# Step products of a prologue in four column groups, and the prologue's order

## The chip, the cores and the metric

The kernel runs on one core of one Trainium2 chip. The metric is the device time of one execution in microseconds (us); less is better. Times of before and after are medians of several runs; the profile is of one more execution.

## What is computed

Sixteen sequences of 512 tokens with 128 features pass through one layer: a state-space mixer, a residual with a layer norm, a mixture of eight experts of which each token takes two, a residual and a layer norm. What matters here is the head of the mixer:

```python
zxbcdt = x @ Win.T
z = zxbcdt[..., :D_INNER]                        # 256 columns
xBC = zxbcdt[..., D_INNER:D_INNER + CONV_DIM]    # 512 columns
dt = zxbcdt[..., D_INNER + CONV_DIM:]            # 4 columns, the steps
xBC = silu(conv(xBC) + conv_b)                   # 4 taps along the tokens
dtp = softplus(dt + dt_bias)
dA = exp(dtp * -exp(A_log))
# then a scan over the tokens, norm, gate, Wout
```

The router's logits `u @ centroids.T` (8 columns) are taken partly from x as well: the kernel folds the part that comes straight from x into the same product, so that the step product of a sequence has 4 + 8 = 12 columns (`DT`).

## The kernel before, in words

Five queues are written out by hand (`block.tensor`, `scalar`, `vector`, `gpsimd`, `sync`), each in its own fixed order, tied by semaphores. Each engine works in program order; what its next instruction waits for holds up all behind it. The work goes in slots: slot -1 is the prologue, slots 0 to 15 each scan one sequence (four chunks of 128 tokens), project the next, and route the one before. Then come 135 expert tiles and the final norm.

The prologue (`enter_all` of TensorE and ScalarE, the first branch of `slot_dve`) has to do three things. It turns all sixteen x blocks: `enter_x(q)` is four transposes on TensorE (L546) into bank p5 or p7, which ScalarE copies to xT (L841). It makes the step products of all sixteen sequences: `enter_dt(q)` on TensorE (L560) has a chunk of xT as the standing operand and `w_dt`, padded from 12 to 96 columns (`PADN`), as the moving one, four chunks a sequence and two passes a chunk, so eight passes. Their results lie in banks p6 (sequences 0 and 1), pl[1] (2 to 9) and p4 (10 to 15), as `dt_place` says; VectorE adds the bias to the four step columns (L1147), and ScalarE copies the eight gate columns (L865, `keep_gates`). And it projects sequence 0: `project_block` (L511) for each of four blocks, ScalarE's first tap (L902, `tap0`), three more taps on VectorE (L1131), `activate` (L908), `skip_part` (L913), z blocks (L519), `gate_part` (L924), `inner_products` (L647), `keep_products` (L919).

The softplus of the steps is fourteen small VectorE instructions in a chain (`softplus_step`, L1161 to L1183), preceded by ScalarE's Abs and Exp (L847, L849). It is done in two groups: sequences 0 and 1 (`G0 = 2`) in the prologue, since the first scans need them, and 2 to 15 in slot 0, five steps after each of its first chunks. `sums` on TensorE (L597), `decay` on ScalarE (L857) and `split` on VectorE (L1196 to L1199) follow each group, then `turn_parts` (L524) and `exponents` (L532 to L537) make the mask exponents of a chunk. Slot 0's first mask is VectorE's L1207: it waits for the inner products' copy and for the exponents.

SyncE issues the x blocks in order (L407 to L415) and loads the expert weights after the second z block. GpSimd makes constants in the prologue.

Of the kernel before, what the change touches and what calls it, by code (L numbers as in the profile page):

```python
# [27 lines left out]
P = 128  # L28
SEQS, TOKS = 16, 512
NC = TOKS // P  # L30
H, HD = 4, 64
# [9 lines left out]
G1 = 10  # L41
# [14 lines left out]
SP_STEPS = 13  # L56
LN_STEPS = 2
GATE_STEPS = 6
G0 = 2
# [6 lines left out]
ON_POOL = 1  # L66
FIN = 4
# [23 lines left out]
def build(nc, t, out):  # L91
    ctx = ExitStack()
    with ctx:
# [17 lines left out]
        w_dt = sb("w_dt", [P, PADN])  # L111
# [167 lines left out]
        gates_in = sem("gates_in")  # L279
        fold_psum = sem("fold_psum")  # L280
# [72 lines left out]
        def dt_place(q):  # L353

            if q < G0:
                return p6, NC * DT * q
            if q < G1:
                return pl[1], NC * DT * (q - G0)
            return p4, P + NC * DT * (q - G1)

        def dt_block(lo, hi):

            o, at = dt_place(lo)
            return o[:, at:at + (hi - lo) * NC * DT].rearrange("p (c e) -> p c e", e=DT)
# [140 lines left out]
        def _(pe):  # L505
# [35 lines left out]
            def enter_x(q):  # L541

                pe.wait_ge(seq_in[q], 16)
                wait(pe, xT_ready, q - 1)
                for c in range(NC):
                    mm = pe.transpose((p5, p7)[q % 2][:, c * P:(c + 1) * P], land[q][:, c, :], ident[:, :])  # L546
                mm.then_inc(xT_psum, 1)

            def enter_dt(q):

                pe.wait_ge(xT_ready, q + 1)
                if q == 0:
                    pe.wait_ge(const_step, 3)
                if q == G1:
                    pe.wait_ge(decays_ready, 1)
                    pe.wait_ge(parts_ready, 1)
                o, first = dt_place(q)
# [43 lines left out]
            def enter_all():  # L601
# [6 lines left out]
                enter_dt(0)  # L608
                project_block(q, 0)
                enter_dt(1)  # L610
                project_block(q, 1)
                enter_x(2)
                for k in range(3, SEQS):
                    enter_x(k)
                    enter_dt(k - 1)
                    if k == 5:
                        pe.wait_ge(const_ready, CONSTS)
                        pe.wait_ge(a_ready, 1)
                        sums(0, G0, (upto, after, ones), 1)
                        project_block(q, 2)  # L620
                    elif k == 7:
                        pe.wait_ge(parts_ready, 1)
                        pe.wait_ge(v_ready, 1)
                        pe.wait_ge(gates_in, 1)
                        turn_parts(q, p6[0:KS, P:2 * P])
                        project_block(q, 3)
                    elif k == 9:
                        pe.wait_ge(picks_made, 1)
                        exponents(q, 0)
                    elif k == 11:  # L630
                        pe.wait_ge(w_in, 16 * W_LOADS)
                        z_block(q, 0)
                enter_dt(SEQS - 1)
                pe.wait_ge(S_ready, 1)
                z_block(q, 1)
                inner_products(q)
                pe.wait_ge(v_ready, 2)
                pe.wait_ge(gates_in, 3)
# [47 lines left out]
            def slot_pe(s, scan, project, route):  # L686
# [4 lines left out]
                for c in range(NC):  # L691
                    tok = slice(c * P, (c + 1) * P)
                    n = NC * s.n + c
                    if scan and c != 1 and (c + 1 < NC or project):
                        if not route and c == 0:
                            pe.wait_ge(v_ready, 2)
                            pe.wait_ge(gates_in, 2)
# [23 lines left out]
                    if project and c == 1:  # L721
                        if q.n == G0:
# [103 lines left out]
        def _(act):  # L826
# [16 lines left out]
            def enter_dt(g, lo, hi):  # L843

                w = (hi - lo) * NC * H
                act.wait_ge(v_ready, g + 1)
                act.activation(ev[:, 0:w], v[:, 0:w], ACT.Abs).then_inc(abs_done, 1)  # L847
# [980 lines left out]
```

## Time and profile before

| | us |
|---|---|
| median of 3 runs | 707.19 |
| the runs | 703.23, 707.2, 707.19 |
| the profiled execution | 704.99 |
| its span, from the first instruction to the last | 703.2 |
| TensorE busy | 638.3 (91%) |
| VectorE busy | 539.3 (77%) |
| ScalarE busy | 478.9 (68%) |
| GpSimd busy | 467.3 (66%) |

All times in rows are us from the span's start. A pass is one MATMUL of the profile; a matmul of 32-bit floats has two, a transpose has one. The engines are called PE (TensorE), ACT (ScalarE), DVE (VectorE), POOL (GpSimd) and SP (SyncE); PEld is the load of the standing operand. A matmul's end is modelled, so in a stream of passes the start-to-start distance is what each costs.

### The profile page before, as it was taken

What the parts mean: (1) busy time and instruction counts of PE and PEld (TensorE: products, weight loads), DVE (VectorE), ACT (ScalarE), POOL (GpSimd) and SP (SyncE); (2) the same over time, 40 slices, a digit from 0 to 9 for tenths busy, and PEclk for the clock granted to TensorE, in tenths of its full rate; (3) what the DMA queues carried; (4) which work ended last, traced back from release to release, by engine and by line L of the source; (5) the groups of instructions that cost most, each with busy time, mean ns of one, the idle gap of its engine ahead of it and who ended that gap; (6) DMA issues with size and microseconds to landing.
All of it is one profiled execution on the core that took longest, in us unless ns stands there. A gap on an engine that the chain in (4) does not pass through costs nothing.

```text
span 703.2 us, 19658 instructions
## 1 busy us (share of the span) xinstructions
PE 638.3 (91%) x4891; PEld 519.3 (74%) x4891; DVE 539.3 (77%) x1845; ACT 478.9 (68%) x1211; POOL 467.3 (66%) x696
## 2 busy tenths in 40 slices
PE   6978999999999999999998689999999999999900
PEld 5856666666666656666666489999999999999900
DVE  3468988889888998889889667776666666878744
ACT  3757778777878778777887367665566556677824
POOL 5012468787878878788777757777745545777754
PEclk9999999999999999999999999999999999999965
DMA  9280001101111011101110123323422223556253
GB/s 251 51 296 20 2 27 36 46 29 35 36 42 47 25 34 35 47 28 38 32 43 32 40 59 86 92 79 108 98 78 72 71 70 102 165 155 190 104 188 111
DMA packets 56668, 54.50 MB, mean 77 GB/s; under 512 B 9562, under 2 KB 45918, under 8 KB 56304
## 3 DMA queue, kind: packets, MB, share of 16 engines
q1 hardware_dynamic: 45840, 33.67, 17.4%
q0 software_dynamic: 8416, 16.93, 7.1%
q10 hardware_dynamic: 2304, 2.65, 1.1%
q8 instruction: 44, 0.72, 0.4%
q14 instruction: 64, 0.52, 0.3%
HBM read 31.05 MB, written 22.63 MB: 76 GB/s over the span
## 4 chain that ended last, share of the span: by engine, by line
PE 69%; issue 8%; POOL 6%; ACT 6%; DVE 5%; DMA 3%; SPq 1%; DVEq 0%; ACTq 0%; POOLq 0%
PE p L682 14%; PE pl L673 10%; PE pj L511 5%; PE p L673 5%; PE p L771 4%; PE p L746 3%; PE p L717 3%; PE p L792 3%; PE p L740 3%; PE p L757 3%; POOL moe_rows L1749 2%; PE pj L519 2%; PE pj L665 2%; PE p L647 2%; PE p L519 1%
## 5 line engine op out<-in xcount | busy, mean ns | idle before, releaser
L1749 POOL DMA_INDIRECT moe_rows<-xT x135 | 134.6, 997 | 79.6 <-DVE xT L1374 51.9
L1673 POOL DMA_INDIRECT sorted_rows<-pair,slot x128 | 128.8, 1007 | 30.6 <-issue 28.4
L1131 DVE SCALAR_TENSOR_TENSOR acc<-pj,conv_w_sb,acc 128x511 f32<-128x511 f32 (+2 forms) x192 | 141.2, 735 | 7.3 <-ACT acc L902 5.3
L682 PE MATMUL p<-w,xT 128*128 x1080 | 143.5, 276 | 3.2 <-ACT xT L1048 3.0
L1048 ACT ACTIVATE xT<-pl,b_sb 128x128 f32<-128x128 f32 x360 | 102.9, 369 | 48.0 <-PE pl L673 46.0
L682 PEld LDWEIGHTS p<-w,xT 128*128 128x128 f32 x1080 | 131.4, 192 | 4.3 <-issue 4.3
L673 PE MATMUL pl<-xT 128*128 128x128 f32 x720 | 95.1, 275 | 1.6 <-DVE xT L1362 1.6
L673 PEld LDWEIGHTS pl<-xT 128*128 128x128 f32 x720 | 87.5, 192 | 1.9 <-issue 1.9
L1370 DVE TENSOR_TENSOR xT<-p,b_sb 128x128 f32<-128x128 f32 x135 | 39.3, 291 | 64.5 <-PE p L682 60.4
L1048 ACT ACTIVATE xT<-p,b_sb 128x128 f32<-128x128 f32 x180 | 51.6, 371 | 23.8 <-PE p L673 23.6
L902 ACT ACTIVATE acc<-pj,conv_b_sb,conv_w_sb 128x512 f32<-128x512 f32 x64 | 49.7, 777 | 25.1 <-PE pj L511 24.2
L511 PE MATMUL pj<-xT,w_xbc 128*128 128x512 f32 x128 | 66.5, 601 | 0.0
L740 PEld LDWEIGHTS p<-M,Xdt 128*64 128x64 f32 x512 | 26.8, 136 | 47.1 <-issue 45.3
L1686 POOL TENSOR_TENSOR Xdd<-Xdt,cur 128x256 f32<-128x256 f32 x48 | 29.5, 615 | 48.0 <-DVE Xdt L1406 34.9
L1362 DVE COPY xT<-w 128x512 f32 x135 | 59.0, 437 | 0.1
L1636 POOL TENSOR_TENSOR gt<-yv,sz 128x256 f32<-128x256 f32 x64 | 47.1, 736 | 11.0 <-DVE yv L1426 10.3
L1207 DVE TENSOR_TENSOR M<-pl,Gm 128x512 f32<-128x512 f32 x64 | 43.9, 686 | 11.6 <-issue 10.1
L1374 DVE SCALAR_TENSOR_TENSOR xT<-xT 128x128 f32<-128x128 f32 x135 | 48.1, 356 | 4.7
L837 ACT ACTIVATE pl<-pl 128x512 f32<-128x512 f32 x64 | 37.2, 582 | 19.5 <-PE pl L537 19.3
L673 PE MATMUL p<-xT 128*128 128x128 f32 x360 | 47.6, 275 | 0.0
L740 PE MATMUL p<-M,Xdt 128*64 128x128 f32 x512 | 42.1, 285 | 5.8 <-issue 4.9
L673 PEld LDWEIGHTS p<-xT 128*128 128x128 f32 x360 | 43.7, 192 | 0.0
(235 smaller groups left out, 1360.6 us busy)
## 6 DMA issues: line engine op xcount, KB each, us to landing
xT<-sorted_rows SPq DMA_DIRECT2D x135, 65.0 KB, 1.9
xres<-in_x SPq DMA_DIRECT2D x16, 256.0 KB, 3.0
w<-in_w SPq DMA_DIRECT2D x2, 2048.0 KB, 10.1
acc<-moe_rows SPq DMA_DIRECT2D x12, 256.0 KB, 3.2
xT<-moe_rows SPq DMA_DIRECT2D x12, 256.0 KB, 5.5
out<-sz ACTq DMA_DIRECT2D x10, 256.0 KB, 2.1
moe_rows<-xT POOLq DMA_INDIRECT x135, 2.5
sorted_rows<-pair,slot POOLq DMA_INDIRECT x128, 2.4
```

Source lines behind the costliest of these rows:

```text
L511: pe.matmul(pj[k % 2][:, :], w_xbc[:, k * P:(k + 1) * P], xT[:, q.n, :], start=True, stop=True).then_inc(proj_psum, 1)
L673: mm = pe.matmul(h_bank[j % 3][:, f * P:(f + 1) * P], w1e[j % 4][:, f * P:(f + 1) * P], sT[j % 4], start=True, stop=True)
L682: mm = pe.matmul(y_bank(j)[:, 0:P], hT[j % 4][:, f, :], w2[:, bass.ds(e, 1), f, :].rearrange("p e d -> p (e d)"), start=(f == 0), stop=(f ...
L740: mm = pe.matmul(p7[half, (h // 2) * P:(h // 2 + 1) * P], Xdt[c % 2][:, h * HD:(h + 1) * HD], M[c % 2][:, h, :], start=(h < 2), stop=(c == ...
L902: act.activation(acc[:, c, :], pj[c % 2][:, :], ACT.Identity, bias=conv_b[:, c:c + 1], scale=conv_w[:, c, TAPS - 1:TAPS]).then_inc(tap0_do ...
L1048: act.activation(hT[j % 4][:, f, :], h_bank[j % 3][:, f * P:(f + 1) * P], ACT.Gelu, bias=b1[:, bass.ds(e * FB + f, 1)]).then_inc(hT_ready, 1)
L1131: ins = dve.scalar_tensor_tensor(out=acc[:, k, j:TOKS], in0=pj[k % 2][:, 0:TOKS - j], scalar=conv_w[:, k, TAPS - 1 - j:TAPS - j], in1=acc[ ...
L1362: dve.tensor_copy(w1e[j % 4], w1[:, bass.ds(expert[j], 1), :].rearrange("p e f -> p (e f)")).then_inc(w1e_ready, 1)
L1374: dve.scalar_tensor_tensor(out=ye[j % 8], in0=ye[j % 8], scalar=xs[k][:, P + 1:P + 2], in1=xs[k][:, 0:P], op0=ALU.mult, op1=ALU.add).then_ ...
L1636: pool.tensor_tensor(gt[:, :, c * P:(c + 1) * P], yv[c % 2][:, :, :], sz[s.par][:, :, c * P:(c + 1) * P], ALU.mult).then_inc(g_ready, 1)
L1673: pool.indirect_dma_start(out=sorted_rows[:, :], out_offset=bass.IndirectOffsetOnAxis(slot[q.par][:, c, k:k + 1], 0), in_=(rowA, rowB)[k][ ...
L1749: pool.indirect_dma_start(out=moe_rows[:, :], out_offset=bass.IndirectOffsetOnAxis(xs[k][:, P:P + 1].bitcast(I32), 0), in_=ye[j % 8], in_o ...
```

## The change

The step product is turned round: `w_dt`, now padded from 12 to 32 columns, stands, and the 512 tokens of a sequence move. Four sequences go into four groups of 32 columns of the array and so to four groups of 32 partitions of one bank, pl[1] (`steps_of`). ScalarE copies the bank to `turned` (`keep_steps`), TensorE turns it in four transposes into p6 (`turn_steps`), and VectorE takes both the steps with their bias and the gates from there. Softplus groups are now sequences 0 to 3 and 4 to 15. The three orders of the prologue are written anew; VectorE copies two of the turned x blocks (13 and 15) in ScalarE's place; nine of the second softplus's fourteen steps stand at the end of the prologue, the other five in slot 0 after chunk 0; Abs and Exp of the second group move from slot 0 to the prologue.

```diff
-G1 = 10
+GROUP = 4
+SP_AHEAD = 9
-G0 = 2
+G0 = GROUP
+X_MOVED = (13, 15)
-        w_dt = sb("w_dt", [P, PADN])
+        w_dt = sb("w_dt", [P, Q])
+        def by_seq(ap):
+            return ap.rearrange("p (c n e) -> p n c e", c=NC, e=Q)
+        def x_turned(eng, n):
+            moved = sum(k < n for k in X_MOVED)
+            wait(eng, xT_ready, n - moved)
+            wait(eng, xT_moved, moved)
 # TensorE
-            def enter_dt(q):
-                pe.wait_ge(xT_ready, q + 1)
...
-                for c in range(NC):
-                    at = first + c * DT
-                    mm = pe.matmul(o[:, at:at + PADN], xT[:, q, c * P:(c + 1) * P], w_dt[:, :],
-                                   start=True, stop=True, skip_group_check=True)
-                mm.then_inc(dt_psum, 1)
+            def steps_of(b):
+                x_turned(pe, GROUP * (b + 1))
+                if b == 0:
+                    pe.wait_ge(const_step, 3)
+                wait(pe, steps_kept, b)
+                for g in range(GROUP):
+                    mm = pe.matmul(pl[1][Q * g:Q * (g + 1), :], w_dt[:, :], xT[:, GROUP * b + g, :],
+                                   start=True, stop=True, skip_group_check=True)
+                mm.then_inc(dt_psum, 1)
+            def turn_steps(b):
+                pe.wait_ge(steps_kept, b + 1)
+                wait(pe, gates_in, b)
+                for c in range(NC):
+                    mm = pe.transpose(p6[:, c * P:(c + 1) * P], turned[:, c * P:(c + 1) * P], ident[:, :])
+                mm.then_inc(dt_psum, 1)
 # TensorE, enter_all, after sum_gates()
+                x_turned(pe, 1)
                 project_block(q, 0)
+                enter_x(2)
+                enter_x(3)
                 project_block(q, 1)
+                enter_x(4)
+                steps_of(0)
+                enter_x(5)
+                turn_steps(0)
+                enter_x(6)
+                project_block(q, 2)
+                enter_x(7)
+                enter_x(8)
+                steps_of(1)
+                project_block(q, 3)
+                turn_steps(1)
+                for k in range(9, 13):
                     enter_x(k)
+                steps_of(2)
+                enter_x(13)
+                turn_steps(2)
+                pe.wait_ge(const_ready, CONSTS)
+                pe.wait_ge(a_ready, 1)
+                sums(0, G0, (upto, after, ones), 1)
+                enter_x(14)
+                pe.wait_ge(parts_ready, 1)
+                turn_parts(q, p4[0:KS, 2 * P:3 * P])
+                enter_x(15)
+                pe.wait_ge(picks_made, 1)
+                exponents(q, 0)
+                pe.wait_ge(w_in, 16 * W_LOADS)
+                z_block(q, 0)
+                steps_of(3)
+                turn_steps(3)
+                pe.wait_ge(gates_in, SEQS // GROUP)
                 z_block(q, 1)
                 inner_products(q)
                 turn_first_x(q)
 # ScalarE
+            def keep_steps(b):
+                act.wait_ge(dt_psum, 2 * b + 1)
+                act.copy(turned[:, :], pl[1][:, :]).then_inc(steps_kept, 1)
 # ScalarE, enter_all, after tap0(q, 0)
+                enter_x(2)
+                enter_x(3)
+                tap0(q, 1)
+                enter_x(4)
+                keep_steps(0)
+                enter_x(5)
                 enter_dt(0, 0, G0)
                 tap0(q, 2)
                 enter_x(6)
                 enter_x(7)
+                enter_x(8)
+                keep_steps(1)
                 tap0(q, 3)
+                for k in range(9, 13):
+                    enter_x(k)
+                keep_steps(2)
+                decay(1, 0, G0, 2, 5)
+                enter_x(14)
+                keep_parts(q, p4[0:KS, 2 * P:3 * P])
                 exp_exponents(0, 0)
                 set_current(q)
+                keep_steps(3)
+                enter_dt(1, G0, SEQS)
                 act.wait_ge(w_in, 16 * W_LOADS)
                 for k in range(XC):
                     activate(q, k)
-                    enter_x(12 + k)
 # VectorE
+            def enter_x(q):
+                dve.wait_ge(xT_psum, q + 1)
+                dve.tensor_copy(xT[:, q, :], (p5, p7)[q % 2][:, :]).then_inc(xT_moved, 1)
 # VectorE, prologue
                     for j in range(1, TAPS):
                         tap(q, 0, j)
+                    tap(q, 1, 1)
+                    enter_dt(0)
+                    tap(q, 1, 2)
+                    tap(q, 1, 3)
                     for k in range(SP_STEPS + 1):
                         softplus_step(0, 0, G0, k)
+                        if k in (1, 4, 7, 10):
+                            tap(q, 2 + k // 10, k // 3 % 3 + 1)
+                    enter_dt(1)
+                    tap(q, 3, 2)
+                    enter_x(13)
+                    enter_dt(2)
                     split(0, 0, G0)
+                    tap(q, 3, 3)
+                    enter_x(15)
                     weigh_out()
+                    enter_dt(3)
+                    for k in range(SP_AHEAD):
+                        softplus_step(1, G0, SEQS, k)
 # VectorE, slot 0
-                    if not route and c + 1 < NC:
-                        for k in range(5 * c, min(5 * c + 5, SP_STEPS + 1)):
+                    if not route and c == 0:
+                        for k in range(SP_AHEAD, SP_STEPS + 1):
                             softplus_step(1, G0, SEQS, k)
```

VectorE's `enter_dt(b)` adds the bias to 64 elements of p6 a partition and copies 128 gate elements to x_logits. GpSimd and SyncE are unchanged.

## Rows read from the trace of the kernel before

**Rows 1.** Chain of waits, 0 to 75 us: start, us, what.

```profile
7.83 1.99 PE p L560 x8
...
17.56 0.87 PE pl L560 x8
...
20.05 0.44 PE p L546 x4
...
34.88 1.82 PE p L560 x16
```

**Rows 2.** Busy time by stage: stretch, length, each engine's us, granted clock, DMA.

```profile
25.00:30.00 5.00, 5.00 (x44) 4.47 (x43) 2.12 (x5) 3.24 (x8) 0.00 (x0) 1.00 0.00 0
39.30:67.60 28.30, 22.56 (x150) 15.93 (x149) 24.54 (x52) 16.61 (x35) 7.04 (x10) 1.00 0.48 179
112.50:135.00 22.50, 22.02 (x150) 14.75 (x149) 20.21 (x65) 17.72 (x37) 18.23 (x31) 1.00 0.12 37
670.00:680.00 10.00, 0.00 (x0) 0.00 (x0) 0.71 (x3) 3.29 (x8) 4.38 (x6) 0.68 0.40 107
```

**Rows 3.** VectorE in order of time, slot 0.

```profile
39.32 0.69 DVE L1207 TENSOR_TENSOR M<-pl,Gm 128x512 f32<-128x512 f32 x1 [1.69 <-issue]
...
42.66 0.27 DVE L1161 TENSOR_SCALAR L<-L 128x224 f32<-128x224 f32 x1
42.97 1.55 DVE L1163 RECIPROCAL L<-L 128x224 f32<-128x224 f32 x1
...
45.60 0.74 DVE L1131 SCALAR_TENSOR_TENSOR acc<-pj,conv_w_sb,acc 128x511 f32<-128x511 f32 x1
...
49.62 2.38 DVE L1171 SCALAR_TENSOR_TENSOR b2e_mem<-b2e_mem 128x224 f32<-128x224 f32 x5
...
55.93 0.80 DVE L1174 SCALAR_TENSOR_TENSOR b2e_mem<-b2e_mem,L 128x224 f32<-128x224 f32 x1
...
67.63 0.69 DVE L1207 TENSOR_TENSOR M<-pl,Gm 128x512 f32<-128x512 f32 x1 [0.51 <-issue]
```

**Rows 4.** TensorE in order of time.

```profile
9.61 1.97 PE L511 MATMUL pj<-xT,w_xbc 128*128 128x512 f32 x2
...
15.65 0.60 PE L546 MATMUL p<-ident,sz 128*128 128x128 f32 x4
...
22.55 1.08 PE L511 MATMUL pj<-xT,w_xbc 128*128 128x512 f32 x2
...
26.07 0.38 PE L532 MATMUL pl<-too_early,ident_b 128*128 128x512 bf16 x1
...
26.73 0.61 PE L546 MATMUL p<-ident,gt 128*128 128x128 f32 x4
...
667.27 2.44 PE L682 MATMUL p<-w,xT 128*128 x16 [0.21 <-ACT xT L1048]
```

**Rows 5.** ScalarE in order of time.

```profile
16.29 0.59 ACT L841 COPY xT<-p 128x512 f32<-128x512 f32 x1 [1.17 <-PE p L546]
...
23.67 0.78 ACT L902 ACTIVATE acc<-pj,conv_b_sb,conv_w_sb 128x512 f32<-128x512 f32 x1 [0.65 <-PE pj L511]
...
61.88 1.28 ACT L908 ACT_TABLE_LOAD   x1
63.18 2.19 ACT L908 ACTIVATE xc<-acc 128x512 f32<-128x512 f32 x4
```

**Rows 6.** TensorE in order of time, 99.6 to 101.2 us, narrow tiles beside full ones.

```profile
99.28 1.02 PE L511 MATMUL pj<-xT,w_xbc 128*128 128x512 f32 x2
100.23 0.66 PE L740 MATMUL p<-M,Xdt 128*64 128x128 f32 x8
100.82 0.60 PE L746 MATMUL p<-ident,carried 128*128 128x128 f32 x3
```

**Rows 7.** The passes of line 740: duration in ns, least, median, most.

```profile
L740 PE MATMUL p<-M,Xdt x512: 272/273/324, 40.5 to 399.6; 128*64 128x128 f32 x171
```

More of the change, by code:

```diff
@@ L543, in enter_x @@
                 pe.wait_ge(seq_in[q], 16)
-                wait(pe, xT_ready, q - 1)
+                x_turned(pe, q - 1)
                 for c in range(NC):
@@ L607, in enter_all @@
                 sum_gates()
-                enter_dt(0)
+                x_turned(pe, 1)
                 project_block(q, 0)
-                enter_dt(1)
+                enter_x(2)
+                enter_x(3)
                 project_block(q, 1)
-                enter_x(2)
-                for k in range(3, SEQS):
-                    enter_x(k)
[L615 to L632, printed above, removed]
@@ L843, in enter_dt @@
             def enter_dt(g, lo, hi):
-                w = (hi - lo) * NC * H
-                act.wait_ge(v_ready, g + 1)
-                act.activation(ev[:, 0:w], v[:, 0:w], ACT.Abs).then_inc(abs_done, 1)
+                e = ev[:, lo * NH:hi * NH]
+                act.wait_ge(v_ready, hi // GROUP)
+                act.activation(e, v[:, lo * NH:hi * NH], ACT.Abs).then_inc(abs_done, 1)
                 act.wait_ge(abs_done, g + 1)
-                act.activation(ev[:, 0:w], ev[:, 0:w], ACT.Exp, scale=-1.0).then_inc(ev_ready, 1)
+                act.activation(e, e, ACT.Exp, scale=-1.0).then_inc(ev_ready, 1)
             def decay(done, lo, hi, first, last):
@@ L931, in enter_all @@
                 tap0(q, 0)
-                enter_dt(0, 0, G0)
-                tap0(q, 1)
-                for k in range(2, 6):
-                    enter_x(k)
-                decay(1, 0, G0, 2, 5)
-                keep_gates(0, G0)
+                enter_x(2)
[4 more added lines that the diff above has]
+                enter_x(5)
+                enter_dt(0, 0, G0)
                 tap0(q, 2)
@@ L940, in enter_all @@
                 enter_x(7)
-                keep_parts(q, p6[0:KS, P:2 * P])
+                enter_x(8)
+                keep_steps(1)
                 tap0(q, 3)
-                enter_x(8)
-                enter_x(9)
+                for k in range(9, 13):
[4 more added lines that the diff above has]
+                keep_parts(q, p4[0:KS, 2 * P:3 * P])
                 exp_exponents(0, 0)
                 set_current(q)
-                for k in range(10, 12):
-                    enter_x(k)
-                keep_gates(G0, G1)
+                keep_steps(3)
+                enter_dt(1, G0, SEQS)
                 act.wait_ge(w_in, 16 * W_LOADS)
@@ L1004, in slot_act @@
                         act.copy(Btok[c % 2][:, :], p5[:, CC * P:(CC + 1) * P]).then_inc(Btok_ready, 1)
-                    if not route and c == 0:
-                        enter_dt(1, G0, SEQS)
                     if s.n == 1 and c == 0:
@@ L1105, in _ @@
             link = chain(const_step, 1)
-            dve.memset(w_dt[:, DT:PADN], 0.0)
+            dve.memset(w_dt[:, DT:Q], 0.0)
             dve.memset(parts[:, :, :], 0.0).then_inc(const_ready, 1)
@@ L1160, in softplus_step @@
                 if k == 0:
-                    ins = dve.tensor_scalar(t1, ev[:, 0:w], 2.0, None, ALU.add)
+                    ins = dve.tensor_scalar(t1, e, 2.0, None, ALU.add)
                 elif k == 1:
```

62 lines of the change are left out of this document (17 added, 45 removed).

## The prediction

> **What bounds the kernel now.** I read the chain of waits first [rows 1]. From 7.8 us to 36.7 us it is TensorE nearly all the way: eight passes of a sequence's step products (L560), four turnings of an x block (L546), now and then a projection, with nothing between. The reader should see that the 16 step products alone are 16 x 0.87 = 13.9 us of a chain of 29. From 40 us on the chain goes over to VectorE. The table of stages [rows 2] says the same: in 25 to 30 us TensorE is busy 5.00 of 5.00 us and VectorE 2.12; from 39.3 to 67.6 us VectorE is busy 24.5 of 28.3 us and TensorE 22.6. So the prologue hangs on TensorE and slot 0 on VectorE. Slot 0 lasts 67.63 - 39.32 = 28.3 us from its first mask (L1207) to slot 1's [rows 3]; later slots come every 22.5 us with TensorE at 22.02 of it [rows 2]. The change touches only what lies before slot 1. I therefore ask two things: when does slot 0's first mask start (before: 39.32), and how long is slot 0 (before: 28.3). All after it should move as one.
>
> **Prices.** On TensorE's path in the prologue [rows 1, 4]: a step product 0.87, an x turning 0.44, a projection or z block 0.88, the six sum passes 0.66, the exponents 0.66 (26.07 to 26.73). From the start of a turning to ScalarE's copy 0.64 (15.65, 16.29); from the start of a projection to its first tap 1.12 (22.55, 23.67) [rows 5]. ScalarE's 512-column copy takes 0.59, and 0.48 apart when they follow one another. VectorE's tap takes 0.74; a softplus step of 224 columns 0.27 to 0.48 (five of L1171 in 2.38), its reciprocal 1.55 [rows 3]. Until about 11.3 us TensorE's passes take twice as long (L511 x2: 1.97 at 9.61, 1.08 at 22.55) [rows 4], that is, the 1.2 GHz level before the 2.4; I keep that moment.
>
> **The new step product.** Four sequences are four matmuls, two passes each of 512 columns, and a pass of 512 is 0.88 / 2 = 0.44. Before: 4 x 0.87 = 3.5 us for four sequences. After, one behind the other: 8 x 0.43 = 3.4, so nothing is won unless the column groups work at once. The only row on that is L740, whose heads go to two column groups, head by head, two passes each [rows 6]. Its eight passes of 128 columns are busy 0.66; less the 0.27 of the last one they start within 0.39. A full-width pass comes every 0.109 (0.44 / 4). One at a time the starts would spread over 7 x 0.109 = 0.76; two abreast over 3 x 0.109 = 0.33, plus 0.05 that the first pass lasts longer (0.324 against 0.273 [rows 7]) = 0.38. So two groups overlap fully. For four groups there is no row: from 2 x 0.43 + some 0.09 = 0.95 (four abreast) through 1.75 (two abreast) to 3.43 (none). I take 0.95, since the one row shows no loss. Narrow and full tiles cost something where they meet: L511's passes at 99.28 are through at 100.16, L740 starts at 100.23, L746 at 100.82, and L746's first three passes take 0.60 where 2 x 0.11 + 0.27 = 0.49 would do; that is 0.07 + (0.59 - 0.44) + 0.11 = 0.33. A call of steps_of is 0.95 + 0.34 = 1.29. Then ScalarE's copy and four transposes of 0.44. In all 1.73 of TensorE for four sequences in place of 3.5: over four groups 7 us less.
>
> The Trainium skill bears on this. In "TensorE: Matmul & The Clock Gate", Part 3 (Packing small matmuls), it gives 2.38x for three column tiles at 512 columns, but says too that matmuls start and end strictly in program order. By that second rule a head's second pass would hold up the next group: 0.05 + 4 x 0.109 = 0.49 of starts at L740, and the row shows 0.39. The trace speaks against the rule; if it held, a call of steps_of would be 5 x 0.43 + 0.34 = 2.5 (second rival).
>
> **The prologue, laid out by these prices.** The 7 us are not all on the path. TensorE now waits for ScalarE, which must copy a product of four (L841's kind, 0.59) before it can be turned, and the order has few others to fill the gap. I went through the three orders line by line; the same walk over the old orders puts the first mask at 39.34 (row: 39.32).
> Up to the first steps_of: projection 0 no longer waits for w_dt and the step product of x0, and starts at 7.5; at half speed it and two turnings take 3.5, then projection 1 and x4: 12.5.
> First to second steps_of: 1.29 + four turnings 1.76 + turn_steps 0.44 + projection 0.88 = 4.4, and waits 1.3 (x8 stands behind ScalarE's tap of block 2, itself behind Abs and Exp): 18.1.
> Second to third: 1.29 + 0.88 + 0.44 + 1.76 = 4.4, waits 0.8: 23.3.
> Third to fourth: 1.29 + three turnings 1.32 + 0.44 + sums 0.66 + turn_parts 0.2 + exponents 0.66 + z 0.88 = 5.45, waits 1.5, of which 1.3 at turn_parts, behind ScalarE's decay and VectorE's four split steps (0.25 each, an estimate from the 224-column steps): 30.3.
> From there no wait can be filled, since ScalarE's order puts Abs and Exp of the last twelve sequences in front of the table load: product 1.21 to ScalarE, copy 0.64, four transposes 0.65, v add 0.3, Abs and Exp 0.7 (an estimate from 512 columns in 0.59), table load 1.28 as before L908 [rows 5], then from the first activate to the mask 67.63 - 63.18 = 4.45 as at the end of slot 0 [rows 3, 5]: 9.3. First mask at 39.6 to 39.9, take 39.7: **0.4 later than before**. Both ends of the unknown: without any of the waits of the first three stretches (3.6) 36.1; each further us in steps_of is passed four times.
> What moves beside it: VectorE takes two turned x blocks (0.6 to 0.7 each, as other 512-column reads of PSUM) and all gates and v adds (eight of 0.2 to 0.3); it has gaps over 1 us ahead of the second, third and fourth. It runs nine of the second softplus's steps (0.27 + 1.35 + 7 x 0.27 to 0.4 = 4.1, for 192 columns) from 33.9 to 38.1, under ScalarE's table load and activates; should that cover go, they push the first mask by what sticks out. x arrives in time: from 25 to 30 us nothing moves (DMA 0.00 [rows 2]), so all sixteen blocks had landed before 25, and the last are needed at 26 and 28. SyncE's w1 and w2 loads follow the two z blocks and start a few us earlier; nobody waits for them before the expert stage. GpSimd's queue has nothing new.
>
> **Slot 0.** Before, three pieces of softplus stand in VectorE's chain: 42.66 to 45.60 (2.9), 49.62 to 51.91 (2.3), 55.93 to 57.81 (1.9) = 7.1 [rows 3]. After, steps 9 to 13 at 192 columns in the first place: 0.35 + 0.7 + 0.25 + 2 x 0.35 = about 2.1. So 5.0 less, if VectorE stays the last. The next late are the carried products and the y sum: by L717 (0.70) and L740 with L746 (1.3), VectorE would idle some 0.15 and 0.3 in the last two chunks. Take **4.6 less**. The change saves ScalarE its Abs and Exp here too, which nobody waited for.
>
> **Sum.** +0.4 - 4.6 = -4.2 us. The profiled execution took 704.99 us (span 703.2), so it would be 700.8. The runs before are 703.23, 707.2 and 707.19: the profiled one lies in between, 2.2 below the median. Against runs as wide as these I set the forecast at 702.0.
>
> **Rivals.**
> First, *the waits are filled*: TensorE's 5.45 and 4.4 are all that counts, since a wait I see is covered by its queue. For: before, TensorE had no gap from 14 to 38 us. Against: before, no product needed a copy by ScalarE ahead of its next step. Up to 3.6 us earlier; 704.99 - 4.2 - 3.6 = 697.
> Second, *groups in strict order*: steps_of 2.5 for 1.29. 4 x 1.2 = +4.8: 705.6, no change. Against it speaks L740's row.
> Third, the other side: *four groups do not overlap at all*, where two do (a shared read of the moving side, say). steps_of is then 3.8, its place is the chain of all four calls, the price 4 x 2.5 = 10 us: 704.99 - 4.2 + 10 = 711, slower. It decides from a call of 1.29 + 4.2 / 4 = 2.3 us on. For: no row has four groups. Against: two show no loss.
> Fourth, *slot 0 gives little back*: the softplus steps stood where VectorE would otherwise wait for TensorE. For: TensorE is busy 22.6 of the 28.3 us [rows 2]. Against: its idle stretches there end on VectorE. Half the 4.6: 703.1.
> Within the first range lies one more: TensorE is idle some 3 us between z block 1 and the inner products. In this trace the granted clock falls (0.68 in 670 to 680 us [rows 2]) after TensorE's last pass ended at 669.7 [rows 4]; a mean of 0.68 between levels of 1 and 0.5 puts the fall at 673.6, 3.9 us behind it. If it fell here, slot 0's first us would run at the lower level, about 2 us.
>
> **How the numbers follow.** Forecast 0.50, first rival 0.20, second 0.12, third 0.08, fourth 0.10. The range reaches from the first rival with a low run (695.5) to just short of the third (709.5). 1% is 7 us, about what a measurement tells from no change. Faster by more: most of the first rival and a tenth of the forecast, 0.23. Slower by more: half of the third and a little of the clock and the second, 0.06. Within 1%: 0.71.
>
> **What would show it.** steps_of's row: eight passes busy 1.1 to 1.3 us, with starts four at a time (right), 2.4 (second rival), 3.6 (third). First mask of slot 0 at 39 to 40.5; slot 1's at 63 to 64.5; slots after it 22.5 apart as before. ScalarE should show gaps of 0.5 to 1.5 us ending on TensorE, and TensorE gaps ending on ScalarE, in 14 to 33 us. The forecast is wrong if the first mask comes before 38 or after 42, or slot 0 is longer than 26 us.

## The result, and the profile after

| | before | after |
|---|---|---|
| median, us | 707.07 (4 runs) | 701.63 (4 runs) |
| the profiled execution, us | 704.99 | 699.86 |
| its span | 703.2 | 698.0 |
| first mask of slot 0 | 39.32 | 39.08 |
| first mask of slot 1 | 67.63 | 62.84 |
| span behind slot 1's first mask | 635.6 | 635.2 |

The ratio is 0.9935 [0.9909, 0.9961]: some 5 us faster, inside the band of 1%. One execution of the kernel after, 826.72 us at a mean clock of 0.745, is left out of the ratio but counted in the median; the median of the other three is 701.54.

A first mask that comes 0.24 us earlier and a slot 0 that is 4.55 us shorter make 4.79 of the 5.2 us of span. The remaining 0.4 lies behind slot 1's mask, where both kernels do nearly the same work. In the fourteen profiled executions of this study that stretch lasted from 633.7 to 637.8 us, without a visible relation to the edits: I take it for noise of an execution, and the last section shows what may be a part of it.

The four new calls, timeline of TensorE in the kernel after (start us, us, engine, line, operation, out<-in, count, idle before and its releaser):

```profile
12.09 1.06 PE L557 MATMUL pl<-xT,w_dt 128*32 128x512 f32 x8
13.08 0.66 PE L547 MATMUL p<-ident,sz 128*128 128x128 f32 x4
...
17.25 0.63 PE L547 MATMUL p<-ident,ysq 128*128 128x128 f32 x4 [1.00 <-ACT xT L851]
17.80 1.06 PE L557 MATMUL pl<-xT,w_dt 128*32 128x512 f32 x8
...
22.87 1.06 PE L557 MATMUL pl<-xT,w_dt 128*32 128x512 f32 x8 [0.19 <-ACT xT L851]
...
27.41 0.26 PE L525 MATMUL p<-ident_b,parts 128*96 128x128 bf16 x1 [1.05 <-DVE parts L1214]
...
29.77 1.07 PE L557 MATMUL pl<-xT,w_dt 128*32 128x512 f32 x8
31.54 0.66 PE L566 MATMUL p<-ident,turned 128*128 128x128 f32 x4 [0.71 <-ACT turned L875]
32.78 1.12 PE L520 MATMUL p<-xT,w_z 128*128 128x512 f32 x2 [0.58 <-DVE x_logits L1162]
36.87 0.38 PE L658 MATMUL p<-xc 128*128 128x128 f32 x1 [2.96 <-ACT xc L917]
```

Eight passes of 512 columns are busy 1.06 us where one behind the other they would take 3.4: the four groups run at once. In the single records of the first call the first four passes start at 12.086, 12.092, 12.099 and 12.106, the second four at 12.539 to 12.559. The next row starts 0.99 behind the call's first pass. The waits of TensorE stand where the prediction put them: 1.00 at x8's turning, 1.05 at the turning of the parts, 0.71 at the fourth product's, 2.96 ahead of the inner products.

VectorE around slot 0's first mask, timeline of the kernel after; it answers to [rows 3]:

```profile
36.11 1.54 DVE L1186 SCALAR_TENSOR_TENSOR b2e_mem<-b2e_mem 128x192 f32<-128x192 f32 x4
39.08 0.69 DVE L1222 TENSOR_TENSOR M<-pl,Gm 128x512 f32<-128x512 f32 x1 [1.44 <-ACT Gm L928]
...
42.53 0.35 DVE L1186 SCALAR_TENSOR_TENSOR b2e_mem<-b2e_mem 128x192 f32<-128x192 f32 x1
42.91 0.36 DVE L1189 SCALAR_TENSOR_TENSOR b2e_mem<-b2e_mem,L 128x192 f32<-128x192 f32 x1
43.30 0.26 DVE L1192 TENSOR_SCALAR tail<-L 128x192 f32<-128x192 f32 x1
43.60 0.36 DVE L1194 SCALAR_TENSOR_TENSOR vals<-b2e_mem,tail 128x192 f32<-128x192 f32 x1
43.99 0.73 DVE L1198 TENSOR_TENSOR vals<-vals,neg_a 128x192 f32<-128x192 f32 x1
44.64 0.74 DVE L1141 SCALAR_TENSOR_TENSOR acc<-pj,conv_w_sb,acc 128x511 f32<-128x511 f32 x1
```

The nine steps done ahead end 1.4 us before the mask, so they are covered; the five that are left occupy 42.53 to 44.64, 2.1 us in place of 7.1.

The table of stages of the kernel after (columns: stretch, length, busy time of PE, PEld, DVE, ACT, POOL with counts, granted clock, DMA share, GB/s); its first two rows answer to the row 39.3:67.6 of [rows 2]:

```profile
39.08:62.84 23.76, 23.24 (x154) 16.39 (x153) 19.91 (x44) 16.17 (x33) 6.97 (x10) 0.96 0.45 158
62.84:85.35 22.51, 21.82 (x148) 14.70 (x147) 19.82 (x61) 17.95 (x37) 8.27 (x13) 1.00 0.04 13
...
36.00:38.00 2.00, 1.13 (x9) 1.13 (x10) 1.51 (x5) 2.00 (x5) 0.00 (x0) 0.95 0.94 385
38.00:42.00 4.00, 4.00 (x20) 1.97 (x18) 1.53 (x3) 3.95 (x8) 0.61 (x1) 0.60 1.05 446
```

In slot 0 VectorE is now busy 19.9 us where it was 24.5, and TensorE 23.24 of 23.76: the slot has gone from the one engine to the other. A part of the 23.24 is only slower passes: in e4 below, where the clock does not fall, TensorE is busy 21.70 of 23.70 us there. The clock column shows the fall that the prediction named as a possibility. TensorE did almost nothing from 33.9 to 36.87, and the mean of 0.60 in 38 to 42 us is mostly the 1.2 GHz level.

ScalarE around the first mask of the kernel after, timeline; the later sections measure from its first activate (34.63) to its copy of Gm (38.43), 3.80 us:

```profile
34.63 2.19 ACT L917 ACTIVATE xc<-acc 128x512 f32<-128x512 f32 x4
...
38.43 0.57 ACT L928 COPY Gm<-p 128x512 f32<-128x512 f32 x1
...
39.51 1.28 ACT L847 ACT_TABLE_LOAD   x1
40.80 0.58 ACT L847 ACTIVATE pl<-pl 128x512 f32<-128x512 f32 x1
```

xc is the output of the conv activates, xD the skip product, sz a gate, and Gm the inner products as the mask takes them.

### The profile page after: what moved, and what is told of

It reads as the page before. It is cut to its first block, busy times and chain, and to the rows that moved or that the text cites. A ratio compares the mean times of both kernels' runs of the same rounds, so it can differ in the third digit from the quotient of the medians.

```text
span 698.0 us, 19510 instructions
## 1 busy us (share of the span) xinstructions
PE 633.0 (91%) x4811; PEld 507.4 (73%) x4811; DVE 542.1 (78%) x1852; ACT 479.5 (69%) x1210; POOL 466.9 (67%) x696
## 4 chain that ended last, share of the span: by engine, by line
PE 62%; issue 11%; POOL 9%; ACT 6%; DVE 5%; DMA 4%; SPq 1%; DVEq 1%; POOLq 0%; ACTq 0%
PE p L693 12%; PE pl L684 8%; PE pj L512 5%; PE p L684 4%; PE p L756 3%; PE p L727 3%; PE p L781 3%; PE p L750 3%; POOL moe_rows L1772 3%; PE p L802 3%; PE p L767 3%; PE pj L520 2%; PE p L658 2%; PE pj L676 1%; PE pl L533 1%
```

## The experiments

No experiment leaves out a part of the computation. Each profile is of one execution, each ratio is to the kernel before on the same chip.

**First, the two halves of the change, and its central mechanism.** e1 is the kernel after with the fourteen steps of the second softplus back in slot 0:

```diff
-                    for k in range(SP_AHEAD):
-                        softplus_step(1, G0, SEQS, k)
...
-                    if not route and c == 0:
-                        for k in range(SP_AHEAD, SP_STEPS + 1):
+                    if not route and c + 1 < NC:
+                        for k in range(5 * c, min(5 * c + 5, SP_STEPS + 1)):
                             softplus_step(1, G0, SEQS, k)
```

> The changed kernel, with none of the second softplus's steps in the prologue: all fourteen in slot 0 again, five after each of the first chunks. Theory (slot 0 gave the time, since nine steps no longer stand in VectorE's chain there): the first mask of slot 0 stays at 39.1 us, since VectorE had 1.4 us to spare ahead of it; slot 0 grows from 23.8 us by the nine steps' 3.9 to 4.2 us to some 27.8; time 703.5 to 704.5 against 699.9 for the changed kernel's own profiled execution. Rival (the prologue and its columns gave the time, the steps were hidden in slot 0 anyway): slot 0 grows by less than 1.5 us, time under 701.5.

e2 is the kernel after with the four narrow matmuls made full-width ones, which can't run side by side:

```diff
+        w_wide = sb("w_wide", [P, GROUP, P])
...
-                    mm = pe.matmul(pl[1][Q * g:Q * (g + 1), :], w_dt[:, :], xT[:, GROUP * b + g, :],
-                                   start=True, stop=True, skip_group_check=True)
+                    mm = pe.matmul(pl[1][:, :], w_wide[:, g, :], xT[:, GROUP * b + g, :],
+                                   start=(g == 0), stop=(g == GROUP - 1), skip_group_check=True)
```

> The changed kernel with the four sequences of a step product one behind the other: the weights stand at full width (128 columns, in which group g holds them at 32 g and zeros stand elsewhere) and four matmuls add up in one bank, same result. Theory (the prologue is a chain that passes through all four calls): a call takes 8 x 0.43 = 3.4 us where it took 1.0 to 1.1, each of the four passes its 2.3 to 2.4 us on, the first mask comes at 48 to 49 us for 39.1; slot 0 stays at 23.8; time 708.5 to 710, slower than the kernel before. Rival (TensorE has waits in the prologue that swallow part of it, 5 us in all): the first mask at 43 to 45 us, time 704 to 706.

e3 is the kernel before with the nine steps, and Abs and Exp, moved ahead, and its old step products; ScalarE's last four x copies and last gate copy, which Abs and Exp need, go ahead of the activates with them (abridged):

```diff
 # ScalarE, prologue: ahead of the four activates
+                enter_dt(1, G0, SEQS)
 # VectorE, end of the prologue
+                    for k in range(9):
+                        softplus_step(1, G0, SEQS, k)
```

> The kernel before, with only one part of the change: Abs and Exp of the second softplus and nine of its steps at the end of the prologue, five in slot 0 after chunk 0. Abs and Exp then stand ahead of ScalarE's table load and activates. Theory (moving the steps only pays because the column groups and the new order end the step products earlier): last product still ends at 36.7 us, then gates, bias, Abs and Exp, table load 1.28 and 4.45 from the first activate: first mask at 43.5 to 44.5 us for 39.3, slot 0 at 24 for 28.3, sum 0 to +0.8 us: 705 to 706 against the profiled 705.0. Rival (the moved steps alone are the gain): first mask under 41 us, 701 to 702.

e4 is the kernel after with three matmuls that nothing reads, in TensorE's idle stretch ahead of the inner products:

```diff
+                for k in range(3):
+                    pe.matmul(pl[1][:, :], ident[:, :], xT[:, k, :], start=True, stop=True,
+                              skip_group_check=True)
                 inner_products(q)
```

> The changed kernel with three more matmuls of 512 columns (results never read) in the gap of TensorE between z block 1 and the inner products, 33.7 to 36.9 us, which in the changed kernel ends with passes twice as long until 41.5. Theory (the fall of the clock costs next to nothing, since ScalarE's table load and exponent hold up chunk 1 of slot 0): the passes after the gap are short again (the inner products 1.05 for 1.26, the projection 1.02 for 1.71), the first mask stays within 0.2 of 39.1, slot 0 at 23.6 to 23.8, time within 0.3 of the changed kernel's. Rival (the lower level costs what its passes cost, 2 us): time 1.5 to 2 us less.

| | first mask | slot 0 | median, us | ratio |
|---|---|---|---|---|
| before, same chip | | | 705.19 | |
| e1 products alone | 40.81 | 28.42 | 704.55 | 0.9982 [0.9963, 1.0001] |
| e2 full width | 50.35 | 24.32 | 712.59 | 1.0107 [1.0062, 1.0152] |
| e3 steps ahead alone | 46.01 | 24.26 | 704.69 | 0.9994 [0.9976, 1.0013] |
| e4 kept busy | 38.97 | 23.70 | 702.12 | 0.994 [0.9919, 0.996] |

e1: slot 0 goes from 23.76 back to 28.42, 4.7 more, and with it most of the gain. Of these 4.66, 0.49 are a wait of VectorE for a slow TensorE (below), so the steps are worth about 4.2. The medians show less: e1's 0.9982 lies 2.8 to 3.3 us above the 0.9935 to 0.9943 of the kernel after and e5, and no run says where the rest goes. Its first mask is 1.7 us later than after's. For 1.15 of this the edit can't be the cause, since it changes no engine's order before 33 us. Timeline of TensorE, kernel after:

```profile
10.70 1.02 PE L512 MATMUL pj<-xT,w_xbc 128*128 128x512 f32 x2
11.56 0.60 PE L547 MATMUL p<-ident,sz 128*128 128x128 f32 x4
```

and e1:

```profile
10.66 1.91 PE L512 MATMUL pj<-xT,w_xbc 128*128 128x512 f32 x2
12.37 0.94 PE L547 MATMUL p<-ident,sz 128*128 128x128 f32 x4
13.24 1.06 PE L557 MATMUL pl<-xT,w_dt 128*32 128x512 f32 x8
```

The same projection, started at the same moment, takes twice as long in e1: its passes are still at the length of the 1.2 GHz level. (The clock column of the stages reads 1.00 here in both kernels, so this first rise is read from the passes.) The first call of `steps_of` starts 1.15 us later. The other 0.58 stand at the inner products, which take 2.08 us in e1 and 1.26 in the kernel after: the clock falls in the idle stretch ahead of them in e1, and a microsecond behind their start (37.8) in the kernel after. 1.15 + 0.58 = 1.73. e2, which keeps the steps in the prologue, has the same 2.08 us, so that part doesn't hang on e1's edit either. First masks of two executions can be compared only with these two things beside them.

e2: timeline of TensorE, first and last call:

```profile
12.95 3.60 PE L559 MATMUL pl<-xT,w_wide 128*128 128x512 f32 x8
...
37.97 3.60 PE L559 MATMUL pl<-xT,w_wide 128*128 128x512 f32 x8
```

A call costs 3.60 in place of 1.06 and the first mask goes to 50.35, 11.27 later. The first call starts 0.86 later (12.95 against 12.09, the clock again), the three stretches from call to call are 2.42, 2.40 and 2.52 longer, and the last, to the mask, 3.07, of which 0.57 are inner products of 2.08 us, as in e1. Each call so passes on 2.4 to 2.5 us, and by the starts of the next operation it costs just that more (3.43 to 3.54 against 0.99 to 1.00): the chain passes on what a call costs in full. The third rival was sized rightly (711 at a call of 3.8), only the chip does not do what it supposes. Without the overlap the change would be a loss of 1%.

e2's slot 0 is 24.32 where the kernel after has 23.76. There TensorE is still at its lower level behind the first mask, and VectorE waits for it (granted clock 0.50 in 52 to 53 us); VectorE's timeline:

```profile
54.02 0.42 DVE L1456 TENSOR_TENSOR yv<-p,xD 128x256 f32<-128x256 f32 x1 [0.57 <-PE p L752]
```

The same wait is 0.49 us in e1 and 0.28 in e3, and it shows in none of the others.

e3: timeline of VectorE:

```profile
38.37 0.29 DVE L1147 TENSOR_TENSOR L<-pl,dt_bias_sb 128x128 f32<-128x128 f32 x1 [9.85 <-ACT x_logits L865]
38.58 0.24 DVE L1147 TENSOR_TENSOR L<-p,dt_bias_sb 128x96 f32<-128x96 f32 x1
39.70 0.28 DVE L1161 TENSOR_SCALAR L<-L 128x224 f32<-128x224 f32 x1 [0.88 <-ACT L L849]
40.02 1.55 DVE L1163 RECIPROCAL L<-L 128x224 f32<-128x224 f32 x1
...
46.01 0.69 DVE L1207 TENSOR_TENSOR M<-pl,Gm 128x512 f32<-128x512 f32 x1 [1.57 <-ACT Gm L919]
```

With the old products the steps of the last sequences are there only at 38.4 us, the activates stand behind them, and the first mask comes at 46.01 where it was 39.32. Of these 6.7 us 0.57 are again inner products of 2.08 us, and 1.2 a late clock (its projection at 13.09 still takes 1.66, and its second z block starts at 37.72 where it was 36.52). So 4.9 us are the price of moving the steps ahead, within what I expected (4.2 to 5.2), and slot 0 gives 4.05 back. So each half alone measures under 0.2%, and both intervals take in no change at all: the new products (e1) buy time that their prologue spends on Abs and Exp of the last sequences ahead of the activates, and the move (e3) gives back in slot 0 what it costs in the prologue. Together they are worth 4 to 5 us. (Its profiled execution of 709.93 is the slowest of its ten.)

e4: table of stages:

```profile
36.00:38.00 2.00, 1.61 (x12) 1.23 (x12) 1.43 (x4) 2.00 (x5) 0.00 (x0) 1.00 0.94 393
38.00:42.00 4.00, 2.91 (x22) 1.40 (x20) 1.65 (x4) 3.97 (x7) 0.61 (x1) 1.00 1.05 446
```

With the gap filled the clock stays at its upper level (1.00 against 0.60) and TensorE does the work of 38 to 42 us in 2.91 us in place of 4.00. And nothing comes of it: first mask 38.97 against 39.08, slot 0 23.70 against 23.76, and the 0.11 of the mask is there before the gap ends (first activate 34.52 against 34.63). ScalarE is busy 3.97 and 3.95 of those 4.00 us: its gates, table load and exponential are the chain there, and the slower TensorE lies beneath them. The one operation whose length can count, the inner products, was nearly through when the clock fell.

**Second, what holds the first mask.** The prediction had said that from the fourth call on "no wait can be filled". In the change's order that holds; the order itself can be another. e5 is the kernel after unchanged. e6 takes the turning of x15 and the fourth call ahead of the wait for the parts, `turn_steps(2)` behind the sums and `turn_steps(3)` ahead of the exponents. ScalarE copies x15, and does Abs and Exp ahead of the exponents' exponential. TensorE's part:

```diff
                 enter_x(13)
-                turn_steps(2)
...
                 sums(0, G0, (upto, after, ones), 1)
+                turn_steps(2)
                 enter_x(14)
+                enter_x(15)
+                steps_of(3)
                 pe.wait_ge(parts_ready, 1)
                 turn_parts(q, p4[0:KS, 2 * P:3 * P])
-                enter_x(15)
+                turn_steps(3)
...
                 z_block(q, 0)
-                steps_of(3)
-                turn_steps(3)
```

> The changed kernel itself, unchanged, as the measure of the three others on the same chip. The start of the higher clock level differs between the profiled executions so far (11.5 us before, 10.5 after, 13.1, 12.5 and 14.3 in three experiments) and moves the first mask with it. Theory: here too the first mask is at 39.1 plus 0.5 to 0.7 us for each us by which the level rises after 10.5; slot 0 is 23.8 whatever that moment; ratio to the kernel before 0.993 to 0.995. Rival (the 0.6% were a chance of four runs): ratio 0.997 or more.

> The changed kernel with another order between the third step product and the second z block: sums ahead of turn_steps(2); x blocks 14 and 15 and the fourth steps_of ahead of turn_parts, so that TensorE does them while ScalarE and VectorE make the parts; ScalarE copies x block 15 itself; Abs and Exp ahead of the exponents' exponential. Theory (the chain from the third call to the first mask is made of waits, 1.05 us at turn_parts and 0.71 at turn_steps(3), and then of ScalarE's 6.5 us): the first mask comes 1.4 to 1.8 us earlier for the same start of the higher clock, slot 0 the same, time 1.4 to 1.8 us under e5. Rival (ScalarE's and VectorE's own work sets that stretch, the order does not matter): within 0.5 us of e5.

e7 is e6 with sequence 0's skip product (L922, twice) on GpSimd in place of ScalarE; e8 is the kernel after with x13 and x15 copied by ScalarE as the other blocks are.

> e6 with sequence 0's two skip products (xD) on GpSimd, which has nothing to do there, in place of ScalarE's 1.22 us between the activates and the gate. Theory (ScalarE's queue is the last from the fourth call to chunk 1): the first mask 0.3 to 0.5 us earlier than in e6 (then the inner products are the last), ScalarE's exponential of chunk 1, and with it slot 0's second mask, 1.2 us earlier; first mask plus slot 0 in all 0.8 to 1.3 us less, time 0.8 to 1.3 under e6. Rival (two GpSimd products of 512 columns at some 1.2 us, beside VectorE on shared memory, come too late for yv or slow VectorE's steps): no less than e6.

> The changed kernel with x blocks 13 and 15 copied by ScalarE again (block 13 after keep_steps(2), block 15 after keep_parts). Theory (ScalarE idles 1.36 us ahead of the decay and 1.0 after keep_parts, waiting for TensorE, and has room for two copies of 0.5): first mask and time within 0.3 us of e5. Rival (the two copies on VectorE are part of the gain): 0.5 to 1 us more than e5.

| | first mask | slot 0 | median, us | ratio |
|---|---|---|---|---|
| before, same chip | | | 706.31 | |
| e5 same again | 39.47 | 23.71 | 701.27 | 0.9943 [0.992, 0.9966] |
| e6 fourth call early | 38.48 | 23.70 | 699.02 | 0.9895 [0.9868, 0.9922] |
| e7 and skip on GpSimd | 38.48 | 23.72 | 699.04 | 0.9902 [0.9875, 0.993] |
| e8 x13, x15 by ScalarE | 39.57 | 23.30 | 701.85 | 0.9927 [0.9899, 0.9955] |

e8 says that VectorE's two copies of turned blocks make no difference that shows. (Its first mask stands 0.4 us late behind its copy of Gm for a reason that the profile doesn't show; its second, 6.86 us behind the first activate, is where the kernel after has it, so the 39.57 and the 23.30 cancel.) e6's first mask is 1.0 us earlier than e5's, where I had expected 1.4 to 1.8. Its first activate is 1.6 earlier (33.44 against 35.02), so the order gained what was expected up to there. Two lines of TensorE and two of ScalarE in e6 say what then holds the mask:

```profile
31.64 1.02 PE L520 MATMUL p<-xT,w_z 128*128 128x512 f32 x2
35.68 2.08 PE L658 MATMUL p<-xc 128*128 128x128 f32 x8 [3.03 <-ACT xc L917]
...
33.44 2.19 ACT L917 ACTIVATE xc<-acc 128x512 f32<-128x512 f32 x4
37.80 0.59 ACT L928 COPY Gm<-p 128x512 f32<-128x512 f32 x1 [0.46 <-PE p L658]
```

In the kernel after, the inner products start at 36.87 and take 1.26; here they start 1.2 earlier and take 2.08, since the clock has fallen before them (0.50 in 36 to 38 us). So the fall that cost nothing in e4's place now seems to lie on the path. e7 gained nothing (38.48 and 699.04, where I had expected 0.8 to 1.3 us less): in e7, whose ScalarE is freed of 1.32 us, ScalarE only waits for TensorE in their place:

```profile
35.73 0.57 ACT L933 ACTIVATE sz<-pj 128x512 f32<-128x512 f32 x1
37.80 0.59 ACT L928 COPY Gm<-p 128x512 f32<-128x512 f32 x1 [1.49 <-PE p L658]
```

**Third, two costs beside each other.** e9 is e6 with e4's three matmuls, e10 is e6 again, e11 is e9 with e7's move, e12 is e9 again.

> The kernel of e6 (fourth step product early) with three unread 512-column matmuls in TensorE's idle stretch, as in e4. In the profile of e6 the inner products take 2.08 us at a granted clock of 0.50 (36:38), against 1.26 in the kernel after, 1.16 in e4; the mask at 38.48 follows the copy of Gm that waits for them. Theory A: in e6, whose chain is shorter, the fall of the clock does lie on the path. Expected: inner products 1.1 to 1.3, first mask 26.0 us behind the rise of the clock instead of 26.7 (so 37.6 to 37.9 where the rise is at 11.8), slot 0 at 23.7, time 0.5 to 1.0 us under e10, about 698.5. Theory B: the fall costs nothing here either, because something else is as late (ScalarE's gates, the table switch at 38.9): first mask 26.5 to 26.8 behind the rise, time within 0.3 us of e10. This run leaves nothing of the computation out; it adds work that nothing reads.

> The kernel of e6 unchanged, on the same chip as e9, for a comparison side by side and for the repeatability of its gain. Expected: 699.0, 0.989 to 0.992 of the kernel before; first mask 26.7 us behind the rise of the clock, slot 0 at 23.7. If the 2.2 us that e6 gained over e5 were a difference between sets of runs, the ratio would be 0.993 to 0.995.

> The kernel of e9 (fourth product early, TensorE kept busy) with sequence 0's xD on GpSimd, as in e7. The copy of Gm ahead of the first mask had two things before it: in e7 ScalarE waited 1.49 us for the inner products (1.89 us at the lower clock level), in e9 the inner products were done and ScalarE was still in xD (1.32 us) and a gate. Theory A: the two costs lie beside each other, so each alone gained nothing and both together gain. Expected: copy of Gm 1.1 to 1.3 us behind the end of the conv activates' last start instead of 2.1, first mask at 37.6 to 37.9 (38.5 in e6, e7 and e9), time 0.5 to 1 us under e12. Theory B: a third thing (the exponents, the x projections) is as late: first mask 38.3 to 38.5 still, time as e12. Nothing of the computation is left out.

> The kernel of e9 unchanged, on the same chip as e11. Expected: first mask at 38.5, time 698.1 within 1 us, ratio to before 0.987 to 0.991.

| | first mask | slot 0 | median, us | ratio |
|---|---|---|---|---|
| e9 e6 and kept busy | 38.52 | 23.69 | 698.11 | 0.9887 [0.9865, 0.9909] |
| e10 e6 again | 38.47 | 23.57 | 699.57 | 0.9924 [0.9902, 0.9946] |
| e11 e9 and skip on GpSimd | 37.21 | 23.70 | 698.15 | 0.9886 [0.986, 0.9911] |
| e12 e9 again | 37.80 | 23.70 | 699.08 | 0.9899 [0.987, 0.9927] |

The rows ahead of the mask, ScalarE in e9:

```profile
34.06 2.19 ACT L920 ACTIVATE xc<-acc 128x512 f32<-128x512 f32 x4
36.16 1.32 ACT L925 ACTIVATE xD<-xc,skip 128x512 f32<-128x512 f32 x2
37.38 0.57 ACT L936 ACTIVATE sz<-pj 128x512 f32<-128x512 f32 x1
37.86 0.57 ACT L931 COPY Gm<-p 128x512 f32<-128x512 f32 x1
```

in e11:

```profile
33.09 2.19 ACT L920 ACTIVATE xc<-acc 128x512 f32<-128x512 f32 x4
35.19 0.57 ACT L936 ACTIVATE sz<-pj 128x512 f32<-128x512 f32 x1
36.53 0.59 ACT L931 COPY Gm<-p 128x512 f32<-128x512 f32 x1 [0.77 <-PE p L661]
```

and the first mask of e11 on VectorE:

```profile
33.80 2.97 DVE L1188 SCALAR_TENSOR_TENSOR b2e_mem<-b2e_mem 128x192 f32<-128x192 f32 x4
37.21 0.69 DVE L1224 TENSOR_TENSOR M<-pl,Gm 128x512 f32<-128x512 f32 x1 [0.44 <-ACT Gm L931]
```

The four steps of L1188 take 2.97 us here where e9's take 1.54, and 2.98 in e7: with the skip product on GpSimd (2.29 us in both) VectorE's steps beside it last nearly twice as long. They still end 0.44 us ahead of the mask (2.22 in e9), so this does not hold the mask, but little of VectorE's spare time is left.

From the start of the four activates to the start of Gm's copy it is a distance that does not hang on when the clock rose, so it is the fair measure of this piece. It is 4.36 in e6 (33.44 to 37.80), 4.03 in e10 (same code; the clock fell later, inner products 1.75) and 4.16 in e7 (1.89), that is, it follows the inner products and xD's place alone gains nothing. It is 3.80 in e9, where ScalarE itself is the last, and 3.44 in e11, where both costs are gone. Keeping TensorE busy alone takes off 0.2 to 0.6, the move of xD 0.36 more, but only with it. That is theory A for e9 and for the move; what theory A of e11 had not seen is that e9 had gained too. Its first mask at 38.52 looks like no gain only because its clock rose late (its projection at 10.86 takes 1.92); e12, the same kernel, has it at 37.80, 0.7 earlier than I expected of it. In time the difference between these versions is not settled: e9 lies 1.46 us under e10 on the same chip, and e12, the same code, has an interval that takes in both e10 and e11. What the times do show is a gain of e6's order over the change's: on one chip its three sets without kept-busy matmuls (e6, e7, e10: 699.02, 699.04, 699.57) all lie under the two of the change's order (e5, e8: 701.27, 701.85), though e10's interval alone would take in e5's ratio. Of the 1.7 to 2.3 us that e6 and e10 lie under e5, the first mask explains about 1; the rest stays unexplained, within what executions differ by.

## Why the prediction was right

The forecast was 702.0 (695.5 to 709.5), the time 701.63, and the mechanisms were those of the forecast. That the two lie within 0.4 us is partly luck: the 702.0 was the sum's 700.8 with 1.2 added for how far the runs before lay apart, and the profiled execution, which the sum was for, took 699.86. The sum gave -4.2 us; the first mask and slot 0 of the profiled pair gave -4.8, the ratio about -4.6. Two of the signs were missed narrowly: a call is busy 1.06 us (1.1 to 1.3 said) and slot 1's first mask is at 62.84 (63 to 64.5 said).

**The call of `steps_of`**: "four abreast" was right, the size a little too high: 1.29 predicted, while the next operation starts 0.99 behind the call's first pass; 0.09 of a gap ahead of it and 0.05 of a slower first pass behind it make 1.14. The switch between tile shapes was the mis-sized term: 0.19 in place of the 0.34 taken from L740; why the two places differ stays open. That second passes of a group don't hold up the next group, read from L740's 0.39 us, was confirmed by the starts at 12.086 to 12.559. The rule of program order that the Trainium skill gives in "TensorE: Matmul & The Clock Gate", Part 3, does not describe what the traces of these two lines show; the time by it (705.6) did not come either.

**The stretches.** From call to call 5.6, 5.2 and 7.0 us were predicted, and 9.3 from the fourth to the mask; 5.71, 5.07, 6.90 and 9.31 were measured. Each of the first three has a call that is 0.15 cheaper than laid out, so the waits in them were longer than laid out, by 0.05 to 0.2: two small errors cancel. The calls themselves lie 0.3 to 0.5 earlier than predicted (12.09 for 12.5, 29.77 for 30.3), nearly all of it from the first stretch: the moment of the clock, which I kept at 11.3, was before 10.7 here. e5, whose projection at 10.89 was still partly slow (1.21), has its first mask at 39.47, beside my 39.7. So "+0.4" against before was right to within this noise, and the -0.24 of the profiled pair says nothing of the change.

**Slot 0.** 4.6 less predicted, 4.55 measured, and e1 gives it back (4.66, of which 0.49 are the clock's).

**The clock in the gap.** "If it fell here, slot 0's first us would run at the lower level, about 2 us." It fell, and e4 shows that it costs 0.1 at most. The step that failed is to price a slower engine by its own extra time (4.00 against 2.91 us busy) without asking who ends last there: ScalarE's 1.28 us table load and the exponential behind it. What it costs depends on when it comes. Behind the start of the inner products it costs the first mask nothing that shows, before them up to 0.57 (e1, e2, e3, e6), and where the lower level lasts into slot 0's first product, another 0.28 to 0.57 there (e1, e2, e3).

**The rivals.** The waits were not filled (1.00, 1.05 and 0.71 us of them stand in the rows), the groups overlap, slot 0 gave all back. The first rival had the sound idea that these waits are there to be had: e6's order brings the first activate 1.6 us forward, and 1.0 of it reaches the mask.

What was not tried: three or two column groups at 512 columns, to find where the overlap begins to cost.

## What to carry to other kernels

Matmuls with a narrow standing operand and few output rows can be put into four column groups, and in a latency chain that turned 3.4 us into 1.1 a call; price it by those rows of the trace, however short, that have any such overlap, and ask at once what the freed time will run into. Here 7 us of TensorE's work gave next to nothing by themselves (0.2%); they paid only together with moving VectorE's work from a stretch where it was the last to one where it waited. A cost counts by who ends last beside it: test two suspected costs together, since each may hide under the other.

## What the runs showed of the hardware that I had not expected

The moment at which TensorE first gets its upper clock differs by 2 us and more between executions of nearly the same instructions: the projection that starts at 10.7 to 10.9 took 1.02 us in the kernel after, 1.21 in e5, 1.91 in e1 and 1.92 in e9, and in e3 one that starts at 13.09 still took 1.66. Between executions of one kernel it moved the first mask by 0.4 (39.08 and 39.47, after and e5) and 0.7 (38.52 and 37.80, e9 and e12).

In four of the fourteen profiles (e3, e5, e6, e8) the clock also fell around 400 us, where slots end and expert tiles begin. Table of stages, e8:

```profile
393.00:403.40 10.40, 9.35 (x41) 7.50 (x40) 3.63 (x22) 0.42 (x1) 7.63 (x9) 0.51 0.36 85
```

and the kernel after:

```profile
393.00:403.40 10.40, 7.12 (x52) 5.68 (x52) 4.02 (x24) 0.42 (x1) 8.97 (x10) 1.00 0.35 79
```

TensorE does fewer operations there in more time. Those four executions have the longest spans behind slot 1's mask, 636.2 to 637.8 us; the ten without it have 633.7 to 636.1. So a part of the spread between runs probably comes from there; no run tests it.

Four column groups have no loss that shows at 512 columns: passes 6 to 8 ns apart, and 0.45 us from the first of a group to its second, the 0.44 of a full-width pass.

TensorE's idle stretch of 2.96 us or more ahead of the inner products came with a fall to the 1.2 GHz level in all nine profiles that have it (after, e1, e2, e3, e5, e6, e7, e8, e10), and in none of the four that fill it (e4, e9, e11, e12). The fall lies between 1.1 us ahead of the end of the idle stretch (e1, where a mean of 0.74 in 36 to 38 us puts it at 36.9 and TensorE starts at 38.02; e3's comes 1.6 ahead, in a stretch of 4.45) and 1.3 us behind it (e5, at 38.6 for a start at 37.26). The time in which it does harm is thus partly a matter of chance.
